# First queries' low parts by VectorE, maxima in two transfers, values around the gelu burst, bias additions moved, unread products in the tail

## The chip, the cores and the metric

The kernel is one program on one of the eight cores of a Trainium2 chip. The metric is the time of one execution on the device in microseconds; the median over runs counts. All engine names are the chip's: TensorE (PE) multiplies into PSUM, VectorE (DVE) and ScalarE (ACT) work elementwise and read PSUM, GpSimd (POOL) works on SBUF alone, SyncE (SP) issues nearly all transfers (DMAs).

## The reference

Four batches of 512 tokens with 256 features go through four residual steps. Each is gated by a tanh and begins with a layer norm. The heart of it:

```
x = x + tanh(g_xattn[0]) * xattn0(layernorm(x), ctx, ctx)     # 16 heads of 16, softmax over 512 keys
x = x + tanh(g_ffn[0])   * moe(layernorm(x))                   # router over 8 experts, the best 2, each x @ W[e]
x = x + tanh(g_xattn[1]) * xattn1(layernorm(x), ctx, ctx)
x = x + tanh(g_ffn[1])   * ffn(layernorm(x))                   # quantised x @ w1.T, gelu, quantised h @ w2.T

q, k, v = query @ Wq.T + bq, key @ Wk.T + bk, value @ Wv.T + bv
out = softmax(q k.T / sqrt(16)) v @ Wo.T + bo
```

The feed-forward network has 1024 hidden features. Weights are rounded to -1, 0 and 1 times a scale, activations to 8 bits with a scale for each token.

## The kernel before, in words

The work is cut into eight passes p = 0 to 7: two layers times four batches. A pass has 16 steps G (four groups of four heads, each in four token tiles), and each step has two halves, so that a pass has 32 slots. `table()` writes out one list for the whole program. In each slot stand: scores `S` of a step six steps ahead (`LEAD`), the transposed scores `T` of this step, whose exponential ScalarE takes (L991), and in every second slot the product with the values `PV` (L782). All other work (projections, layer norms, output projection, router and experts, feed-forward) is put into slots by hand in `work_table()`: `put(p, s, ...)` puts it into slot s of pass p. Every engine walks through the same list and executes its own part of each entry, in this order and never in another. So each engine has a fixed queue, and semaphores hold it at each entry until its inputs are there.

Queries and keys are split into a high part and a low part, so that products of them are exact enough. `SPLIT` does this for 128 features of a projection: TensorE multiplies (L707), ScalarE writes a full copy `qf` (L938) and a rounded high part (L939), GpSimd subtracts one from the other for the low part (L574), and SP stores both to the scratch tensors `qd` or `kd`. `RELOAD` brings them back from there, arranged by heads, as `qs` and `ks` (L521).

The softmax needs the maximum of each row. VectorE takes it from the scores (L1171, 512 reductions in the program). For each group of heads GpSimd splits the maxima into two parts (`M`, L648, L651), TensorE transposes them (`MT`, L791), ScalarE copies them (L1007), and SP moves them with four transfers into rows of `qs` (L531), for each part and each half of the partitions one. The transposed product `T` (L768) then subtracts them by itself.

`VV` (L727, L1125) makes the values of the next pass. In passes 5 to 7 all four gelu products `F1` (L879, L1042) of the previous batch stand together in slot 16, since ScalarE has to load another function table for the gelu and load the exponential's table after it (1.28 us each). They use the PSUM tiles of the scores, `psT` for the even ones and `psS` for the odd ones, and the scores wait until the gelus have read them. In passes 5 and 6 two `VV` stand among them; pass 7 has none.

`BIAS` adds the output projection's bias, scaled by the gate, to the residual `xs` on GpSimd (L621); `BOB` scales that bias on VectorE (L1087). After pass 7 comes a tail for the last batch alone: output projection (L819), layer norm, quantisation `XQ` and `XI`, transposes `XB` (L858), four gelu products, and for each of four tiles the rounding `HQ`, `HS`, transposes `HT` (L889) and the second product `F2` (L897).

The bookkeeping that the change touches on TensorE is the table of what frees each of the two banks of `psX`, which all the small work shares in turn:

```
freed = {"WS": (v_scale, 1, 1), "SPLIT": (a_split, 2, 2), "VV": (v_vv, 1, 1), "XT": (a_xt, 1, 1), "OT": (a_ot, 1, 1),
```

Of the kernel before, what the change touches and what calls it, by code (L numbers as in the profile page):

```python
# [19 lines left out]
F32 = mybir.dt.float32  # L20
F32R = mybir.dt.float32r
# [60 lines left out]
def work_table():  # L82
# [16 lines left out]
    put(lead, 24, ("BOB", ()))  # L99
    put(lead, 25, ("BIAS", (0, 0)))  # L100
# [3 lines left out]
    put(0, 0, ("SPLIT", ("Q", 1, 0)), ("LD", ("x3",)), ("BIAS", (1, 0)))  # L104
# [7 lines left out]
    put(0, 8, ("VV", (1, 0)), ("BIAS", (2, 0)), ("LD", ("moe0",)))  # L112
# [6 lines left out]
    put(0, 14, ("VV", (1, 1)), ("BIAS", (3, 0)))  # L119
# [16 lines left out]
    for p in range(1, NP):  # L136
# [35 lines left out]
        else:  # L172
# [19 lines left out]
    put(NP, 5, ("XQ", (0, 2)), ("LNN", (b, 2, 4)), ("XI", (0, 2)), ("XB", (0, 2)), ("XQ", (2, 4)), ("XI", (2, 4)))  # L192
    put(NP, 5, ("F1", (0,)), ("XB", (2, 4)), ("F1", (1,)), ("F1", (2,)), ("F1", (3,)))
# [56 lines left out]
def build(nc, x, ctxT, g_xattn, g_ffn, Wq, bq, Wk, bk, Wv, bv, Wo, bo, rw, rb, ew, w1, w2, out):  # L250
    with ExitStack() as ctx:
# [143 lines left out]
        v_xn = sem("v_xn")  # L395
        v_norm = sem("v_norm")
# [27 lines left out]
        for kind, args in table():  # L424
            if kind == "SPLIT":
                split_no[args] = len(split_no)

# [16 lines left out]
        def _(sp):  # L444
# [52 lines left out]
            def split(what, p, c):  # L497
                i = n("SPLIT")
                at, pr = (kd if what == "K" else qd)[p], parts[:, i % 2]
                if due(p_split, i + 1):  # L500
                    sp.wait_ge(p_split, i + 1)
# [22 lines left out]
            def max_rows(g):  # L524
# [21 lines left out]
        def _(pool):  # L546
# [23 lines left out]
            def split(what, p, c):  # L570
                i = n("SPLIT")
                if due(a_split, 2 * (i + 1)):
                    pool.wait_ge(a_split, 2 * (i + 1))
# [95 lines left out]
        def _(pe):  # L669
# [3 lines left out]
            freed = {"WS": (v_scale, 1, 1), "SPLIT": (a_split, 2, 2), "VV": (v_vv, 1, 1), "XT": (a_xt, 1, 1), "OT": (a_ot, 1, 1),  # L673
# [17 lines left out]
            def split(what, p, c):  # L691
                l = p // B
                o = bank("SPLIT")
                if what == "Q":
# [703 lines left out]
```

## Time and profile before

| | us |
|---|---|
| median of 3 runs | 766.89 |
| fastest and slowest of them | 765.59 and 769.69 |
| the profiled execution | 766.51 |
| its span, first to last instruction | 764.7 |
| TensorE busy in it | 676.7 (88%) |
| VectorE busy | 530.5 (69%) |
| ScalarE busy | 446.8 (58%) |
| GpSimd busy | 167.0 (22%) |
| mean granted clock of TensorE | 0.960 of full |

The profiled execution is one run; all lengths and times within the program come from it, counted from the span's start. A busy TensorE is not one at its peak, because products overlap and their ends are modelled. The engines run side by side: a length counts towards the time only where the others wait for it.

### The profile page before, as it was taken

What the parts mean: (1) busy time and instruction counts of PE and PEld (TensorE: products, weight loads), DVE (VectorE), ACT (ScalarE), POOL (GpSimd) and SP (SyncE); (2) the same over time, 40 slices, a digit from 0 to 9 for tenths busy, and PEclk for the clock granted to TensorE, in tenths of its full rate; (3) what the DMA queues carried; (4) which work ended last, traced back from release to release, by engine and by line L of the source; (5) the groups of instructions that cost most, each with busy time, mean ns of one, the idle gap of its engine ahead of it and who ended that gap; (6) DMA issues with size and microseconds to landing.
All of it is one profiled execution on the core that took longest, in us unless ns stands there. A gap on an engine that the chain in (4) does not pass through costs nothing.

```text
span 764.7 us, 10140 instructions
## 1 busy us (share of the span) xinstructions
PE 676.7 (88%) x3550; PEld 323.6 (42%) x3554; DVE 530.5 (69%) x1138; ACT 446.8 (58%) x572; POOL 167.0 (22%) x302
## 2 busy tenths in 40 slices
PE   4799999998999999998999989998889789987746
PEld 2433333344544445444554445443344344432324
DVE  3467876578886688868787688864786768775234
ACT  2227666773346633664336734468776778568746
POOL 6325222630010310121101410113210311021132
PEclk9769999999999999999999999999999999969987
DMA  7848578512120601123220321216032312200000
GB/s 239 230 117 317 180 232 267 158 34 52 42 43 29 166 18 26 46 108 84 43 43 30 122 47 42 43 70 207 10 83 64 94 39 64 43 2 9 21 0 28
DMA packets 39922, 66.74 MB, mean 87 GB/s; under 512 B 6080, under 2 KB 14784, under 8 KB 39616
## 3 DMA queue, kind: packets, MB, share of 16 engines
q1 hardware_dynamic: 39024, 65.57, 30.0%
q8 instruction: 28, 0.46, 0.3%
q10 hardware_dynamic: 848, 0.53, 0.2%
q14 instruction: 22, 0.18, 0.1%
HBM read 38.29 MB, written 27.26 MB: 86 GB/s over the span
## 4 chain that ended last, share of the span: by engine, by line
PE 56%; DVE 14%; ACT 12%; issue 9%; POOL 6%; DMA 2%; SPq 0%; POOLq 0%; DVEq 0%; ACTq 0%
PE psO L782 10%; PE psS L754 7%; PE psX L707 7%; DVE mx L1171 6%; PE psT L768 6%; PE psX L843 5%; PE psX L819 4%; ACT pt L991 4%; PE psX L844 4%; PE psX L845 4%; PE psX L727 3%; ACT qf L938 2%; DVE xs L1302 2%; POOL parts L574 2%; ACT parts L939 2%
## 5 line engine op out<-in xcount | busy, mean ns | idle before, releaser
L991 ACT ACTIVATE pt<-psT 128x1024 f32<-128x1024 f32 x256 | 261.8, 1023 | 217.1 <-PE psT L768 214.7
L1171 DVE TENSOR_REDUCE mx<-psS 128x1 f32<-128x512 f32 x512 | 325.1, 681 | 87.4 <-PE psS L754 86.1
L754 PE MATMUL psS<-ks,qs 48*128 48x512 f32 x512 | 153.8, 516 | 18.9 <-DVE mx L1171 13.2
L782 PE MATMUL psO<-pt,vg 128*32 128x512 f32 x1024 | 140.4, 621 | 0.1
L768 PE MATMUL psT<-qs,ks 50*128 50x512 f32 x512 | 118.2, 431 | 9.6 <-ACT pt L991 8.2
L754 PEld LDWEIGHTS psS<-ks,qs 48*128 48x128 f32 x512 | 61.0, 191 | 138.2 <-issue 72.3
L1302 DVE SCALAR_TENSOR_TENSOR xs<-psX,coef,xs 128x256 f32<-128x256 f32 x128 | 61.8, 483 | 31.8 <-PE psX L845 28.5
L574 POOL TENSOR_TENSOR parts<-qf,parts 128x512 fp32r<-128x512 f32 x32 | 40.8, 1275 | 158.7 <-ACT parts L939 158.7
L768 PEld LDWEIGHTS psT<-qs,ks 50*128 50x128 f32 x512 | 52.2, 189 | 29.4 <-ACT pt L991 25.8
L843 PE MATMUL psX<-moeh,xh 128*128 128x512 f32 x128 | 57.1, 446 | 5.3 <-DVE xs L1302 5.3
L844 PE MATMUL psX<-moel,xh 128*128 128x512 f32 x128 | 50.7, 396 | 0.0
L845 PE MATMUL psX<-moeh,xl 128*128 128x512 f32 x128 | 50.2, 392 | 0.0
L843 PEld LDWEIGHTS psX<-moeh,xh 128*128 128x128 f32 x128 | 23.9, 187 | 43.9 <-DVE xs L1302 23.8
L707 PE MATMUL psX<-ctxb,wk 128*128 128x512 f32 x64 | 34.4, 667 | 7.7 <-DMA wk<-in_Wk 7.7
L648 POOL CAST mp<-mx 128x16 fp32r<-128x16 f32 x32 | 6.4, 199 | 158.6 <-DVE mx L1171 157.7
L948 ACT ACTIVATE xn<-xs,lnw 128x256 f32<-128x256 f32 x60 | 31.8, 591 | 14.2 <-POOL lnw L610 14.1
L663 POOL TENSOR_SCALAR hh<-hh,am 128x1024 f32<-128x1024 f32 x16 | 18.0, 1123 | 95.2 <-DVE am L1343 95.2
L782 PEld LDWEIGHTS psO<-pt,vg 128*32 128x32 f32 x1024 | 20.3, 108 | 43.5 <-issue 42.5
L707 PE MATMUL psX<-xnt,wq 128*128 128x512 f32 x64 | 32.2, 630 | 1.3 <-ACT xnt L961 0.8
L819 PE MATMUL psX<-wo,ont 128*128 128x256 f32 x128 | 31.6, 391 | 0.8 <-ACT ont L984 0.8
L1100 DVE BATCH_NORM_STATS2 st<-xs 128x6 f32<-128x256 f32 x64 | 26.4, 413 | 7.4 <-DMA xs<-in_x 6.7
L1125 DVE TENSOR_TENSOR vg<-psX,bvb 128x512 f32<-128x512 f32 x16 | 11.0, 691 | 29.1 <-PE psX L727 29.1
(128 smaller groups left out, 748.9 us busy)
## 6 DMA issues: line engine op xcount, KB each, us to landing
ks<-kd SPq DMA_DIRECT2D x64, 192.0 KB, 3.7
qs<-qd SPq DMA_DIRECT2D x64, 192.0 KB, 4.5
kd<-parts SPq DMA_DIRECT2D x16, 512.0 KB, 3.1
qd<-parts SPq DMA_DIRECT2D x16, 512.0 KB, 2.7
kd<-parts SPq DMA_DIRECT2D x16, 256.0 KB, 3.8
qd<-parts SPq DMA_DIRECT2D x16, 256.0 KB, 3.7
ctxb<-in_ctxT SPq DMA_DIRECT2D x7, 512.0 KB, 3.5
xs<-in_x SPq DMA_DIRECT2D x4, 512.0 KB, 6.4
```

The source lines that it names most:

```text
L574: g.tensor_tensor(parts[:, i % 2, 1, :].bitcast(F32R), qf[:, i % 2, :], parts[:, i % 2, 0, :], ALU.subtract).then_inc(p_split, 1)
L707: i = mm(o, w[:, k, c * P:(c + 1) * P], src[:, k, :], start=k == 0, stop=k == NC - 1)
L754: mm(psS[:, i % 3, :], qs[at:at + KR, 2 * g + a, k * P:(k + 1) * P], ks[at:at + KR, 2 * g + a, :], start=True, stop=True).then_inc(pe_s, 1)
L768: i = mm(psT[:, r, :], ks[at:at + KR + MP, 2 * g + half, k * P:(k + 1) * P], qs[at:at + KR + MP, 2 * g + half, :], start=True, stop=True)
L782: i = mm(psO[32 * j:32 * j + 32, :], vg[:, p % 2, k, g * GH + j, :], pt[:, s % RING, j, :], start=k == 0, stop=k == NT - 1, tile_position= ...
L819: i = mm(o[:, t * D:(t + 1) * D], ont[:, k, tt * P:(tt + 1) * P], wo[l][:, k, :], start=k == 0, stop=k == NC - 1)
L843: mm(o, xh[:, k, tok], moeh[:, k, at], start=k == 0, stop=False)
L844: mm(o, xh[:, k, tok], moel[:, k, at], start=False, stop=False)
L845: i = mm(o, xl[:, k, tok], moeh[:, k, at], start=False, stop=k == NC - 1)
L991: a(pt[:, G % RING, 2 * half:2 * half + 2, :], psT[:], ACT.Exp, scale=SCALE).then_inc(a_exp, 1)
L1171: v.tensor_reduce(mx[:, w // GH % 2, r, col:col + 1], psS[:, i % 3, :], AX.X, ALU.max).then_inc(v_max, 1)
L1302: v.scalar_tensor_tensor(out=xs[:, b, t, :], in0=o[:, k * D:(k + 1) * D], scalar=coef[:, t, e:e + 1], in1=xs[:, b, t, :], op0=ALU.mult, op ...
```

## The change

It has five parts.

1. The low parts of the first pass's queries (`SPLIT` with ("Q", 0, 0) and ("Q", 0, 1)) are made by VectorE straight from PSUM: product plus bias minus high part, in one instruction. ScalarE's full copy and GpSimd's subtraction are left out for these two.
2. The transposed maxima of a group go to `qs` with two transfers in place of four. Each writes one row in both halves of the partitions.
3. In passes 5 and 6 one `VV` stands ahead of the four gelu products and one behind them.
4. `BOB` moves from slot 24 to slot 31 of the lead-in, and the four `BIAS` of layer 0 from slots 25 of the lead-in, 0, 8 and 14 of pass 0 to slots 5, 13, 21 and 29 of pass 0.
5. In the tail TensorE makes 46 products of 128x512 (29, 4, 4 and 9) whose result no one reads.

```diff
-    put(lead, 24, ("BOB", ()))
-    put(lead, 25, ("BIAS", (0, 0)))
+    put(lead, 31, ("BOB", ()))
...
+    for b in range(B):
+        put(0, 5 + 8 * b, ("BIAS", (b, 0)))
...
-            for t in range(NT):
-                put(p, 16, ("F1", (t,)))
-                if p < NP - 1 and t in (1, 2):
-                    put(p, 16, ("VV", (p + 1, t - 1)))
+            burst = [("F1", (t,)) for t in range(NT)]
+            if p < NP - 1:
+                burst = [("VV", (p + 1, 0))] + burst + [("VV", (p + 1, 1))]
+            put(p, 16, *burst)
...
-    put(NP, 5, ("XQ", (0, 2)), ("LNN", (b, 2, 4)), ("XI", (0, 2)), ("XB", (0, 2)), ("XQ", (2, 4)), ("XI", (2, 4)))
-    put(NP, 5, ("F1", (0,)), ("XB", (2, 4)), ("F1", (1,)), ("F1", (2,)), ("F1", (3,)))
+    put(NP, 4, ("BUSY", (29,)))
+    put(NP, 5, ("XQ", (0, 2)), ("LNN", (b, 2, 4)), ("XI", (0, 2)), ("XB", (0, 2)), ("BUSY", (4,)), ("XQ", (2, 4)), ("XI", (2, 4)))
+    put(NP, 5, ("F1", (0,)), ("XB", (2, 4)), ("BUSY", (4,)), ("F1", (1,)), ("F1", (2,)), ("F1", (3,)),
+        ("BUSY", (9,)))
...
                 for k in range(MP):
-                    for half in range(2):
-                        row, src = HALF * half + KR + k, k * GH * NT + half * 2 * NT
-                        sp.dma_start(qs[row:row + 1, 2 * g:2 * g + 2, :].bitcast(F32)
-                                     .rearrange("p h (t q) -> p (h t) q", q=P),
-                                     mt[src:src + 2 * NT, i % 2, :]).then_inc(d_m[i % 2], 16)
+                    sp.dma_start(qs[KR + k:HALF + KR + k + 1:HALF, 2 * g:2 * g + 2, :].bitcast(F32)
+                                 .rearrange("p h (t q) -> p (h t) q", q=P),
+                                 mt[k * GH * NT:(k + 1) * GH * NT, i % 2, :]).then_inc(d_m[i % 2], 16)
...
+                last[b] = (v_split, dve_parts(i + 1)) if by_dve(i) else (a_split, act_parts(i + 1))
...
+            def keep_busy(k):
+                if due(a_oe, n("OE")):
+                    pe.wait_ge(a_oe, n("OE"))
+                if due(v_quant, 16):
+                    pe.wait_ge(v_quant, 16)
+                for i in range(k):
+                    mm(psO[:], identb[:], w1q[:, 0, 0:S], start=True, stop=True)
...
-                a(qf[:, i % 2, :], o, ACT.Identity, bias=bias).then_inc(a_split, 1)
+                if not by_dve(i):
+                    if due(p_split, pool_parts(i - 1)):
+                        act.wait_ge(p_split, pool_parts(i - 1))
+                    a(qf[:, i % 2, :], o, ACT.Identity, bias=bias).then_inc(a_split, 1)
                 a(parts[:, i % 2, 0, :].bitcast(F32R), o, ACT.Identity, bias=bias).then_inc(a_split, 1)
...
+                if due(pe_split, i + 1):
+                    dve.wait_ge(pe_split, i + 1)
+                if due(a_split, act_parts(i + 1)):
+                    dve.wait_ge(a_split, act_parts(i + 1))
+                v.scalar_tensor_tensor(out=parts[:, i % 2, 1, :].bitcast(F32R), in0=bank(), scalar=bqc[:, 0, c:c + 1],
+                                       in1=parts[:, i % 2, 0, :], op0=ALU.add, op1=ALU.subtract).then_inc(v_split, 1)
```

`by_dve(i)` is true for the two splits of part 1; `dve_parts`, `pool_parts` and `act_parts` count the instructions that each engine has made up to a split.

What the change moves on the engines, in the order in which their instructions stand (line numbers are each program's own). First VectorE in the opening, before the change, from the normalised first batch (`xn`) over the second batch's statistics (`st`, `mv`) to the maxima (`mx`):

```order
L1111 TENSOR_SCALAR xn<-xs,lnw 128x256 x4
L1100 BN_STATS st<-xs 128x6
L1105 BN_AGGR mv<-st 128x2
...
L1125 TENSOR_TENSOR vg<-psX,bvb 128x32x16 x2
L1171 TENSOR_REDUCE mx<-psS 128x1 x10
L1087 TENSOR_SCALAR bob<-bob,gt 128x256 x2
L1171 TENSOR_REDUCE mx<-psS 128x1 x16
```

And after the change, at the same place:

```order
L1144 TENSOR_SCALAR xn<-xs,lnw 128x256 x4
L1171 SCALAR_TENSOR_TENSOR parts<-psX,bqc,parts 128x512
L1133 BN_STATS st<-xs 128x6
L1138 BN_AGGR mv<-st 128x2
...
L1171 SCALAR_TENSOR_TENSOR parts<-psX,bqc,parts 128x512
L1158 TENSOR_TENSOR vg<-psX,bvb 128x32x16 x2
L1215 TENSOR_REDUCE mx<-psS 128x1 x24
L1120 TENSOR_SCALAR bob<-bob,gt 128x256 x2
L1215 TENSOR_REDUCE mx<-psS 128x1 x2
```

The first low part has come ahead of the four pairs of statistics, the second between them and the values, and the scaling of the bias has moved from behind the 10th maximum to behind the 24th.

Next TensorE at the gelu burst of pass 5, before the change (`xit` are the transposed inputs, `wv,ctxb` a `VV`):

```order
L768 MATMUL psT<-qs,ks 128x512 x2
L879 MATMUL psT<-w1q,xit 128x512 x4
L879 MATMUL psS<-w1q,xit 128x512 x4
L727 MATMUL psX<-wv,ctxb 128x256 x4
L879 MATMUL psT<-w1q,xit 128x512 x4
L727 MATMUL psX<-wv,ctxb 128x256 x4
L879 MATMUL psS<-w1q,xit 128x512 x4
L754 MATMUL psS<-ks,qs 128x512 x2
```

And after it:

```order
L792 MATMUL psT<-qs,ks 128x512 x2
L751 MATMUL psX<-wv,ctxb 128x256 x4
L903 MATMUL psT<-w1q,xit 128x512 x4
L903 MATMUL psS<-w1q,xit 128x512 x4
L903 MATMUL psT<-w1q,xit 128x512 x4
L903 MATMUL psS<-w1q,xit 128x512 x4
L751 MATMUL psX<-wv,ctxb 128x256 x4
L778 MATMUL psS<-ks,qs 128x512 x2
```

The two projections of values have gone from among the gelu products to both sides of them.

Last TensorE in the tail, where before the change the transposes of the quantised inputs (`identb,xi`) follow the output projection at once:

```order
L819 MATMUL psX<-wo,ont 128x256 x8
L858 MATMUL psX<-identb,xi 128x128 x4
L879 MATMUL psT<-w1q,xit 128x512 x4
L858 MATMUL psX<-identb,xi 128x128 x4
L879 MATMUL psS<-w1q,xit 128x512 x4
```

And after it:

```order
L843 MATMUL psX<-wo,ont 128x256 x8
L930 MATMUL psO<-w1q,identb 128x512 x29
L882 MATMUL psX<-identb,xi 128x128 x4
L930 MATMUL psO<-w1q,identb 128x512 x4
L903 MATMUL psT<-w1q,xit 128x512 x4
L882 MATMUL psX<-identb,xi 128x128 x4
L930 MATMUL psO<-w1q,identb 128x512 x4
L903 MATMUL psS<-w1q,xit 128x512 x4
```

The unread products (`psO<-w1q,identb`) have come in between; nine more stand behind the last gelu product.

## Rows read from the trace of the kernel before

**Rows 1.** The page: the clock in 40 slices, and the chain that ended last by engine.
```profile
PEclk9769999999999999999999999999999999969987
...
PE 56%; DVE 14%; ACT 12%; issue 9%; POOL 6%; DMA 2%; SPq 0%; POOLq 0%; DVEq 0%; ACTq 0%
```

**Rows 2.** The chain that ended last, opening of the program: start us, us, what.
```profile
19.98 1.28 POOL parts L574
...
29.61 0.84 PE psS L754 x2
...
36.42 0.60 DVE bob L1087 x2
```

**Rows 3.** Timeline, 14 to 29 us: start, length, engine, line, operation, idle before it.
```profile
14.52 0.41 DVE L1100 BATCH_NORM_STATS2 st<-xs 128x6 f32<-128x256 f32 x1
...
16.55 0.18 DVE L1105 BATCH_NORM_AGGREGATE mv<-st 128x2 f32<-128x6 f32 x1
...
19.22 0.68 ACT L939 ACTIVATE parts<-psX,bqc 128x512 fp32r<-128x512 f32 x1
...
26.43 1.07 PE L738 MATMUL psX<-identf,xn 128*128 128x128 f32 x8 [2.67 <-ACT xn L948]
```

**Rows 4.** Groups by shape, VectorE: count, busy us, mean ns, idle before.
```profile
L1198 DVE SCALAR_TENSOR_TENSOR xs<-psX,gt,xs 128x512 f32<-128x512 f32 x16 | 12.0, 748 | 24.6 <-PE psX L819 24.6
```

**Rows 5.** Timeline, maxima moved and first products that read them, 42 and 211 us.
```profile
42.03 2.84 SPq L531 DMA_DIRECT2D qs<-mt  x4
...
46.06 0.29 PEld L768 LDWEIGHTS psT<-qs,ks 50*128 50x128 f32 x2 [0.19 <-DMA qs<-mt]
...
211.59 2.69 SPq L531 DMA_DIRECT2D qs<-mt  x4
...
221.62 0.40 PE L768 MATMUL psT<-qs,ks 50*128 50x512 f32 x2
```

**Rows 6.** Timeline, gelu burst of pass 6, with values inside.
```profile
609.01 1.02 ACT L991 ACTIVATE pt<-psT 128x1024 f32<-128x1024 f32 x1
...
611.83 1.89 PE L727 MATMUL psX<-wv,ctxb 128*128 128x256 f32 x8
...
618.91 1.29 DVE L1171 TENSOR_REDUCE mx<-psS 128x1 f32<-128x512 f32 x2 [1.88 <-PE psS L754]
...
619.63 1.03 ACT L991 ACTIVATE pt<-psT 128x1024 f32<-128x1024 f32 x1
```

**Rows 7.** Busy us by stretch: PE, PEld, DVE, ACT, POOL, PEclk, DMA share, GB/s.
```profile
620.00:640.00 20.00, 17.46 (x129) 8.17 (x127) 19.09 (x41) 16.18 (x19) 3.79 (x5) 1.00 0.23 55
```

**Rows 8.** Timeline, gelu burst of pass 7, without values.
```profile
687.86 1.02 ACT L991 ACTIVATE pt<-psT 128x1024 f32<-128x1024 f32 x1
...
692.37 1.04 PE L879 MATMUL psS<-w1q,xit 128*128 128x512 bf16 x4
...
694.58 1.28 ACT L991 ACT_TABLE_LOAD   x1
```

**Rows 9.** Timeline, the same exponential in passes 6 and 7.
```profile
597.07 1.02 ACT L991 ACTIVATE pt<-psT 128x1024 f32<-128x1024 f32 x1 [1.22 <-PE psT L768]
...
673.64 1.02 ACT L991 ACTIVATE pt<-psT 128x1024 f32<-128x1024 f32 x1 [1.22 <-PE psT L768]
```

**Rows 10.** The chain of the tail, 724 to 765 us, by line.
```profile
by line: PE psX L897 8.9%; ACT hh L1042 7.9%; PE psT L879 7.0%; issue 6.9%; ACT hq L1053 5.3%; PE psX L889 5.1%; PE psX L819 4.8%; PE psS L879 4.5%; POOL lnw L594 3.6%; ACT hqt L1067 3.6%; PE psO L782 2.7%; ACT xit L1031 2.7%; ACT ont L984 
```

**Rows 11.** Timeline, TensorE's long pause in the tail.
```profile
730.20 3.69 PE L819 MATMUL psX<-wo,ont 128*128 128x256 f32 x16 [0.83 <-ACT ont L984]
...
741.32 0.59 PE L858 MATMUL psX<-identb,xi 128*128 128x128 bf16 x4 [7.43 <-ACT xi L1021]
```

**Rows 12.** Busy us by stretch, columns as in Rows 7.
```profile
674.00:688.00 14.00, 13.11 (x53) 4.41 (x45) 8.50 (x17) 8.95 (x13) 3.23 (x11) 0.52 0.01 2
...
739.00:749.00 10.00, 5.23 (x18) 2.32 (x20) 3.46 (x13) 5.54 (x8) 3.27 (x7) 0.50 0.01 2
```

**Rows 13.** Timeline, one bias addition on GpSimd.
```profile
52.58 2.34 POOL L621 TENSOR_TENSOR xs<-xs,bob 128x1024 f32<-128x1024 f32 x1
```

More of the change, by code:

```diff
@@ L103, in work_table @@
         st(0, 5 + t, 3, t)
-    put(0, 0, ("SPLIT", ("Q", 1, 0)), ("LD", ("x3",)), ("BIAS", (1, 0)))
+    put(0, 0, ("SPLIT", ("Q", 1, 0)), ("LD", ("x3",)))
     put(0, 1, ("LD", ("w1",)))
@@ L118, in work_table @@
     put(0, 13, ("WS", ()))
-    put(0, 14, ("VV", (1, 1)), ("BIAS", (3, 0)))
+    put(0, 14, ("VV", (1, 1)))
     pair(0, 16, "SPLIT", "Q", 3, step=2)
@@ L395, in build @@
         v_xn = sem("v_xn")
+        v_split = sem("v_split")
         v_norm = sem("v_norm")
@@ L426, in build, with by_dve, dve_parts, pool_parts @@
                 split_no[args] = len(split_no)
+        def by_dve(i):
+            return i in (split_no["Q", 0, 0], split_no["Q", 0, 1])
+        def dve_parts(i):
+            return sum(by_dve(k) for k in range(i))
+        def pool_parts(i):
+            return i - dve_parts(i)
+        def act_parts(i):
+            return 2 * i - dve_parts(i)
         def ctx_of(p):
@@ L499, in split @@
                 at, pr = (kd if what == "K" else qd)[p], parts[:, i % 2]
-                if due(p_split, i + 1):
-                    sp.wait_ge(p_split, i + 1)
+                if by_dve(i):
+                    if due(v_split, dve_parts(i + 1)):
+                        sp.wait_ge(v_split, dve_parts(i + 1))
+                else:
+                    if due(p_split, pool_parts(i + 1)):
+                        sp.wait_ge(p_split, pool_parts(i + 1))
                 if what == "Q":
@@ L571, in split @@
                 i = n("SPLIT")
-                if due(a_split, 2 * (i + 1)):
-                    pool.wait_ge(a_split, 2 * (i + 1))
+                if by_dve(i):
+                    return
+                if due(a_split, act_parts(i + 1)):
+                    pool.wait_ge(a_split, act_parts(i + 1))
                 g.tensor_tensor(parts[:, i % 2, 1, :].bitcast(F32R), qf[:, i % 2, :], parts[:, i % 2, 0, :],
@@ L692, in split @@
                 l = p // B
+                i = n("SPLIT")
+                b = n.piece() % 2
                 o = bank("SPLIT")
+                last[b] = (v_split, dve_parts(i + 1)) if by_dve(i) else (a_split, act_parts(i + 1))
                 if what == "Q":
@@ L759, in t_pair @@
                 if k == 0 and half == 0:
-                    if due(d_m[no % 2], 64 * (no // 2 + 1)):
-                        pe.wait_ge(d_m[no % 2], 64 * (no // 2 + 1))
+                    if due(d_m[no % 2], 32 * (no // 2 + 1)):
+                        pe.wait_ge(d_m[no % 2], 32 * (no // 2 + 1))
                 if due(a_exp, n("T")):
@@ L1004, in mt_ @@
                     act.wait_ge(pe_mt, i + 1)
-                if due(d_m[i % 2], 64 * (i // 2)):
-                    act.wait_ge(d_m[i % 2], 64 * (i // 2))
+                if due(d_m[i % 2], 32 * (i // 2)):
+                    act.wait_ge(d_m[i % 2], 32 * (i // 2))
                 a(mt[:, i % 2, :].bitcast(F32R), bank()[0:MP * GH * NT, 0:P], ACT.Copy).then_inc(a_mt, 1)
@@ L1128, in vv, with split @@
                                 ALU.add).then_inc(v_vv, 1)
+            def split(what, p, c):
+                i = n("SPLIT")
+                if not by_dve(i):
+                    return
+                if due(pe_split, i + 1):
+                    dve.wait_ge(pe_split, i + 1)
+                if due(a_split, act_parts(i + 1)):
+                    dve.wait_ge(a_split, act_parts(i + 1))
+                v.scalar_tensor_tensor(out=parts[:, i % 2, 1, :].bitcast(F32R), in0=bank(), scalar=bqc[:, 0, c:c + 1],
+                                       in1=parts[:, i % 2, 0, :], op0=ALU.add, op1=ALU.subtract).then_inc(v_split, 1)
             def raw(k):
@@ L1354, in f2 @@
                                        in1=xs[:, b, t, :], op0=ALU.mult, op1=ALU.add).then_inc(v_f2, 1)
-            walk({"BOB": scale_bo, "ST": stats, "LNV": normalise, "VV": vv, "ABS": abs_sum, "WS": scales, "QUANT": quant, "S": maxima,
+            walk({"BOB": scale_bo, "ST": stats, "LNV": normalise, "SPLIT": split, "VV": vv, "ABS": abs_sum, "WS": scales, "QUANT": quant, "S": maxima,
                   "NT": norm, "OP": op, "R1": router1, "R2": router2, "R3": router3, "R4": router4, "ME": experts, "XQ": xq,
```

8 lines of the change are left out of this document (3 added, 5 removed).

## The prediction

> **What bounds the kernel now.** I read the page first. The chain that ended last spends 56% of the span on TensorE, 14% on VectorE, 12% on ScalarE and 6% on GpSimd, and the clock row shows TensorE at its upper level (2.4 GHz) nearly everywhere [rows 1]. It is lower in slices 2 and 3 (the opening), in slice 36 (669 to 688 us) and in the last two (the tail). So the steady passes belong to TensorE, and a saving of waits counts only where TensorE itself stands still or runs at 1.2 GHz. Of the change's places, four could be such: the opening, the two gelu bursts that carry value projections, the transfers of the maxima, and the tail.
>
> In the opening the chain runs over GpSimd's subtraction for the first queries, their store, their reload, and the first scores at 29.61 [rows 2]. Then VectorE's maxima set the pace, with BOB's two scalings (0.60) between them, up to the first transposed product at 46.06 [rows 2, 5]. In the tail TensorE stands idle for 7.43 us before the transposes at 741.32, and works at a granted clock of 0.50 from 739 to 749 [rows 11, 12].
>
> **First queries' low parts.** The subtraction ended at 21.26 (19.98 + 1.28) [rows 2]. Now ScalarE writes one copy instead of two. Its high part takes 0.68 [rows 3] and can start where the full copy did, some 0.6 before 19.22, thus ends at 19.3. VectorE then adds the bias and subtracts. The same kind of instruction on 128x512 out of PSUM takes 0.75 [rows 4], so it ends at 20.1. The store leaves 1.2 earlier.
>
> VectorE executes in order, and this instruction stands before the second batch's statistics, which ran from 14.52 to 16.73 in VectorE's free time [rows 3]. They now run from 20.1 to 22.3. Their normalisation on GpSimd could start at 21.3, behind the subtraction [rows 2]; it now starts at 22.3, about 1.0 later. What hangs on it is the transposes at 26.43 (1.07 long) [rows 3]: they move to 27.4 and end at 28.5. TensorE issues the first scores behind them. These were at 29.61; the store would allow 28.4, the transposes allow 28.55. **Gain 1.05**, with 1.2 as the upper end. The cover (2.1 us between transposes and scores) is then used up; the lower end is 0.5, if the statistics or the normalisation run later by as much again. The second low part stands behind those statistics, holds its PSUM bank until 23 and delays the second value projection, which has until 27.4.
>
> **BOB and the bias additions.** BOB leaves the place between the 10th and 11th maximum and stands behind the 24th. There the first transposed product may already start, and TensorE next does a projection while VectorE has two maxima left. **Gain 0.6** [rows 2]. The four additions on GpSimd cost 2.34 each [rows 13], the same number as before. They move to slots 5, 13, 21 and 29 of pass 0, each just behind the splitting of a group's maxima (slots 3, 11, 19, 27) and so as far as can be from the next. There they stand ahead of one low-part subtraction each; the first also waits for ScalarE's normalisation. What waits behind them is that subtraction and its store, and ScalarE only two projections later. I take 0. Without that cover each would cost up to 2.34.
>
> **Maxima in two transfers.** SP issues 128 transfers now and 64 after. Four take 2.69 to issue [rows 5], so two should take 1.35. Who waits? In a steady pass the four are issued by 214.3 and the first product that reads their rows comes at 221.62 [rows 5], a cover of 7.3 us. The saving there is worth 0. Only the very first group is near: issued 42.03 to 44.87, and the product at 46.06 was released by that landing, 1.2 after the last issue [rows 5]. VectorE's chain reaches the same point within 0.2. Both gates move: the maxima are ready 1.65 earlier, and issuing is done 1.4 earlier still. So the first product should follow VectorE's chain; between 0 and 0.2 more.
>
> The row shows four transfers landing 1.2 after the last issue. The Trainium skill's page DMA: Bandwidth & Descriptors (section on why a DMA increments its semaphore by 16) says that the number of engines is the largest up to 16 that divides the slowest dimension of both sides. By it the old form (8 rows on each side) used eight engines, and the new one (2 partitions against 16 rows) uses two, each with eight rows in a line. By that rule issuing gets cheaper and landing slower; no row here times the new form. By the row alone the sum has 0 for this edit, by the rule anything up to the whole 7.3 cover would still be 0, and only the first group could lose some tenths.
>
> **Values at both ends of the burst.** Pass 6 has two projections inside, pass 7 has none. I count from the start of the last exponential. In pass 7 the last gelu ends 6.72 later (694.58 - 687.86) [rows 8]. In pass 6 the next exponential, which comes 1.28 plus a few hundredths after the last gelu, starts 10.62 later (619.63 - 609.01) [rows 6], so the last gelu ends 9.3 later. The two projections inside cost ScalarE 2.6. Now the first stands before the first gelu product: it can start when the last transposed product ends, runs some 1.73 (1.89 with the filling of the array [rows 6]) while ScalarE still has its exponential (1.02) and the table load (1.28), and makes the first gelu 0.25 late. The second stands behind the last product, which in pass 7 ends 5.55 after the exponential's start (692.37 + 1.04 - 687.86) [rows 8]. So it ends at 5.55 + 0.25 + 1.73 = 7.5, and scores and transposed products follow (0.40 for such a pair [rows 5], so 0.7 to 0.8). They are ready at 8.25, the table at 6.72 + 0.25 + 1.28 = 8.25, and the exponential starts at 8.27. **ScalarE gains 10.62 - 8.27 = 2.35.** VectorE has a copy out of PSUM to make before its next maximum (0.75 by [rows 4]), so that starts at 7.5 + 0.75 = 8.25 and not at 9.90 (618.91 - 609.01) [rows 6]: **gain 1.65**. In the 20 us that follow VectorE is busy for 19.09, ScalarE for 16.18 [rows 7], so VectorE sets most of the pace. I take 1.8 for each, **3.6 for the two** (passes 5 and 6), between 3.3 and 4.7.
>
> **Unread products in the tail.** Twenty-nine products follow the output projection, which ends at 733.9 [rows 11], in the pause. Four of this size took 1.04 at the upper level [rows 8], so 29 take 6.3 to 7.5 and end at 740.2 to 741.4. The transposes want TensorE at 741.3. They cost about nothing if the clock is still up when they begin. On the chain of the tail (40.7 us) the gelu products are 7.0 + 4.5%, or 4.7 us; the transposes of the hidden rows 5.1%, or 2.1; the last products 8.9%, or 3.6 [rows 10]. At the upper level two gelu products stand before a gelu, 2.1 instead of 4.7, and one more gelu of 1.1 joins the chain: -1.5. The small transposes and weight loads around them give 0.5. In the second half -0.9 for transposes and -0.7 for one product at the lower level; ScalarE then sets the pace and takes back 0.6. **Gain 3.0**, of 3.6 at most. The groups of 4 and 4 stand ahead of a first product and of a second one, whose inputs come from ScalarE a short copy later; at 0.9 each, 0.2 of delay is in the sum. The 9 at the end (1.9) hide behind two gelus. The lower end is 1.0, if the clock falls again before the last products.
>
> **Sum.** 1.05 + 0.6 + 0 + 0 + 3.6 + 3.0 = 8.25. The profiled execution took 766.5 (its span 764.7 plus 1.8 around it) and the median of the runs is 766.9. So 758.3 against the profiled one, and **758.6** for the median.
>
> **Rivals.**
> 1. The tail does not gain (chance 0.14). The clock falls before the products come, or they start at the lower level, where 29 take twice as long, up to 12.6, and end at 746.5, 5 us after the transposes want the engine. For it: they only keep up what is there, and the tail ahead of them has gaps [rows 11]. Against: the projection before them is 3.7 us without a gap at the upper level. Gain 0 to -3 in the tail: 762 to 765.
> 2. The bursts give little (0.08), if TensorE or VectorE takes back the time in the following pass: 766.9 - 1.65 - 3.0 - 0.5 = 761.8. Against it stands pass 7, where the burst without projections is 2.6 shorter.
> 3. The dips fall elsewhere (0.12 with an effect over 2 us). From 674 to 688 TensorE ran at 0.52 though it was busy for 13.11 of 14 [rows 12]; pass 6 at the same place ran at full clock. The same two exponentials lie 11.94 apart in pass 6 and 14.22 in pass 7 [rows 6, 8, 9]: a dip costs 2.3 or more, since pass 7 also lacks a projection (1.9). All the work shifts against it here. Without it 755 to 756, with one more 761 to 763.
> 4. The maxima come too late (0.03), the case on the other side: two engines carrying sixteen rows one after the other, behind the reloads. It decides from a landing 7.3 + 1.35 us later than now [rows 5]; from there on each microsecond costs one for each of 32 groups. A landing 9 us later gives 766.9 - 8.25 + 32 x 0.35, or 770.
>
> The forecast itself has 0.63. **Range 754.5 to 762.5**: below it the lost dip, above it the case without the tail's gain. What this kernel's measurement tells from no change is about 0.5%, 3.8 us. Over 763.1 is only the bad half of rival 1, part of 4, and several losses at once: faster 0.90, same 0.07, slower 0.03.
>
> **What would show it.** The first scores near 28.5 and the first transposed product near 44.4. The last exponential before the table load and the next one 8.3 apart in passes 5 and 6, with no gap in TensorE ahead of the third gelu product. SP's groups of two near 1.35 and no wait of transposed products for them. Clock 1.00 from 739 on and the last gelu about 2 us nearer to the transposes. I am wrong if scores come after 29.2, if the unread products end after 741.5, or if a new dip stands in pass 5 or 6.

## The result, and the profile after

The changed kernel takes **763.94 us** (median of 20 runs, 757.05 to 769.72), the kernel before 768.4 beside it (20 runs, 764.61 to 770.45). The ratio is **0.9945, 95% interval 0.9923 to 0.9967**, or 4.2 us less where I forecast 8.25. The forecast of 758.6 stood on 766.89, the median of three runs of the kernel before; beside the changed kernel that median is 768.4, so 1.5 of the 5.3 us between 758.6 and 763.94 come from the base, and the rest is gain that did not come. I call "low time" the time at TensorE's lower level: two times (1 - mean granted clock) times 765 us. It is 56 us as a mean over the runs of after (two slow ones left out, as in all ratios) and 63 over the 35 runs of before that stand beside e1 to e4 below.

First the opening, by the timeline of TensorE and then of ScalarE in the kernel after (start, length, what ran, in brackets the idle time ahead and what ended it). These answer to [rows 2, 3 and 5].

```profile
27.47 1.06 PE L762 MATMUL psX<-identf,xn 128*128 128x128 f32 x8 [2.48 <-ACT xn L981]
28.49 1.22 PE L778 MATMUL psS<-ks,qs 48*128 48x512 f32 x3
...
43.96 1.21 PE L792 MATMUL psT<-qs,ks 50*128 50x512 f32 x2
45.11 3.78 PE L731 MATMUL psX<-xnt,wq 128*128 128x512 f32 x4
```

```profile
48.92 0.69 ACT L971 ACTIVATE qf<-psX,bqc 128x512 f32<-128x512 f32 x1 [2.69 <-PE psX L731]
```

The scores start at 28.49 (29.61 before). The first two transposed products start at 43.96 and end at 45.17, where before they ended at 46.86, so that the exponential behind them comes 1.7 earlier. The projection behind them runs at 1.2 GHz for its whole 3.78 (3.18 before), so part is given back: the same copy stood at 50.01 before and is 1.1 earlier now.

The burst of pass 6, by the timelines of ScalarE, VectorE and TensorE of after, answering to [rows 6]:

```profile
610.04 1.02 ACT L1024 ACTIVATE pt<-psT 128x1024 f32<-128x1024 f32 x1
611.08 1.28 ACT L1075 ACT_TABLE_LOAD   x1
...
617.09 1.28 ACT L1024 ACT_TABLE_LOAD   x1
618.38 1.02 ACT L1024 ACTIVATE pt<-psT 128x1024 f32<-128x1024 f32 x1
```

```profile
617.68 0.69 DVE L1158 TENSOR_TENSOR vg<-psX,bvb 128x512 f32<-128x512 f32 x1 [5.15 <-PE psX L751]
618.29 1.28 DVE L1215 TENSOR_REDUCE mx<-psS 128x1 f32<-128x512 f32 x2
619.48 1.21 DVE L1377 TENSOR_REDUCE am<-hh 128x1 f32<-128x1024 f32 x1
...
621.30 1.28 DVE L1215 TENSOR_REDUCE mx<-psS 128x1 f32<-128x512 f32 x2
```

```profile
620.67 0.49 PE L778 MATMUL psS<-ks,qs 48*128 48x512 f32 x1
622.04 0.53 PE L778 MATMUL psS<-ks,qs 48*128 48x512 f32 x1 [0.88 <-DVE mx L1215]
622.04 0.96 PE L792 MATMUL psT<-qs,ks 50*128 50x512 f32 x2
622.93 1.93 PE L806 MATMUL psO<-pt,vg 128*32 128x512 f32 x8
```

From exponential to exponential it is 8.34 (618.38 - 610.04; 8.33 in pass 5), where I forecast 8.27 and before had 10.62. But VectorE, idle for 5.15 inside the burst, now has the copy of the values, two maxima and the first hidden tile's quantisation maximum (`HQ`, L1377) in a row. TensorE waits 0.88 for it, where before it waited 0.32, and the product with the values at 622.93 takes 1.93 instead of 1.06: the clock has fallen. The same two places in the trace before:

```profile
622.67 0.50 PE L754 MATMUL psS<-ks,qs 48*128 48x512 f32 x1 [0.32 <-DVE mx L1171]
...
623.34 1.06 PE L782 MATMUL psO<-pt,vg 128*32 128x512 f32 x8
```

The fall shows in the windows of after (busy time of each engine with the number of instructions, then the granted clock):

```profile
616.00:619.00 3.00, 3.00 (x20) 1.56 (x18) 1.32 (x3) 2.97 (x4) 0.00 (x0) 1.00 0.00 0
619.00:622.00 3.00, 2.03 (x13) 0.97 (x9) 2.90 (x8) 1.99 (x3) 0.52 (x1) 1.00 0.01 3
622.00:625.00 3.00, 2.96 (x13) 0.70 (x15) 2.36 (x5) 1.96 (x2) 1.02 (x3) 0.56 0.00 0
625.00:628.00 3.00, 3.00 (x17) 1.71 (x17) 2.31 (x3) 2.04 (x4) 0.00 (x0) 0.50 0.00 0
```

Pass 5 is the same in kind: a pause of 0.88 ahead of 542.81, then low clock from 544, for 3.4 us instead of the 6.8 of pass 6. The trace before had no low stretch behind either burst.

The tail, by the timeline of TensorE after and one window, answering to [rows 11, 12]:

```profile
732.99 3.69 PE L843 MATMUL psX<-wo,ont 128*128 128x256 f32 x16 [0.83 <-ACT ont L1017]
736.73 6.21 PE L930 MATMUL psO<-w1q,identb 128*128 128x512 bf16 x28
744.09 0.38 PE L882 MATMUL psX<-identb,xi 128*128 128x128 bf16 x4 [1.15 <-ACT xi L1054]
```

```profile
739.00:749.00 10.00, 8.13 (x43) 3.41 (x42) 4.07 (x13) 5.68 (x9) 4.42 (x15) 1.00 0.00 0
```

The clock is 1.00 where it was 0.50. From the output projection to the last instruction on VectorE it is 29.8 us (732.99 to 762.80) against 32.4 (730.20 to 762.58): 2.6 gained. At the places touched the opening gains 1.1, each burst 1.65 (VectorE's next maximum) and the tail 2.6, and yet the span is that of before (764.9 and 764.7). What a burst gains can be followed further, to the first exponential of the next pass. From the last exponential ahead of the table load to that one it was 41.49 in pass 5 (530.89 to 572.38) and 41.47 in pass 6 (609.01 to 650.48). It is now 40.59 (530.81 to 571.40) and 42.06 (610.04 to 652.10): of the 3.3 of the two bursts 0.3 is left there. The 17 us of low time that stood in the tail are gone, but the mean granted clock is 0.958 against 0.960, so as much stands elsewhere. One such stretch, of 6.8 us from 595, lies in pass 6 ahead of its burst and makes the way there 2.0 longer (38.64 from 571.40 to 610.04, against 36.63 before). Over the runs of after, time and low time go together (correlation 0.95): each us of low time goes with 0.34 us.

### The profile page after: what moved, and what is told of

Same layout as the page of the kernel before. It is cut to its first block, busy times and chain, and to the rows that moved or that the text cites. A ratio compares the mean times of both kernels' runs of the same rounds, so it can differ in the third digit from the quotient of the medians.

```text
span 764.9 us, 10167 instructions
## 1 busy us (share of the span) xinstructions
PE 691.0 (90%) x3595; PEld 327.5 (43%) x3600; DVE 533.3 (70%) x1140; ACT 445.5 (58%) x570; POOL 164.3 (21%) x300
## 4 chain that ended last, share of the span: by engine, by line
PE 59%; DVE 14%; ACT 11%; issue 9%; POOL 8%; POOLq 0%; DVEq 0%; ACTq 0%
PE psO L806 11%; PE psS L778 8%; PE psX L731 7%; PE psT L792 6%; PE psX L867 5%; DVE mx L1215 5%; PE psX L843 4%; PE psX L868 4%; PE psX L869 4%; PE psX L751 3%; ACT pt L1024 3%; POOL parts L595 2%; DVE xs L1346 2%; ACT qf L971 2%; ACT parts L972 1%
## 5 line engine op out<-in xcount | busy, mean ns | idle before, releaser
L806 PE MATMUL psO<-pt,vg 128*32 128x512 f32 x1024 | 142.0, 627 | 0.1
L1346 DVE SCALAR_TENSOR_TENSOR xs<-psX,coef,xs 128x256 f32<-128x256 f32 x128 | 61.8, 483 | 32.4 <-PE psX L869 29.2
L595 POOL TENSOR_TENSOR parts<-qf,parts 128x512 fp32r<-128x512 f32 x30 | 38.4, 1280 | 152.5 <-ACT parts L972 152.5
L731 PE MATMUL psX<-ctxb,wk 128*128 128x512 f32 x64 | 36.6, 705 | 7.3 <-DMA wk<-in_Wk 7.3
L751 PE MATMUL psX<-wv,ctxb 128*128 128x256 f32 x128 | 33.0, 403 | 0.8 <-DVE parts L1171 0.8
L612 POOL TENSOR_SCALAR lnw<-mv 128x4 f32<-128x4 f32 (+1 forms) x17 | 3.9, 229 | 126.3 <-DVE mv L1138 125.7
```

What stands on the lines that cost most here:

```text
L731: i = mm(o, w[:, k, c * P:(c + 1) * P], src[:, k, :], start=k == 0, stop=k == NC - 1)
L751: i = mm(o[:, t * D:(t + 1) * D], ctxb[:, p % 2, k, (2 * half + t) * P:(2 * half + t + 1) * P], wv[l][:, k, :], start=k == 0, stop=k == NC ...
L806: i = mm(psO[32 * j:32 * j + 32, :], vg[:, p % 2, k, g * GH + j, :], pt[:, s % RING, j, :], start=k == 0, stop=k == NT - 1, tile_position= ...
L1346: v.scalar_tensor_tensor(out=xs[:, b, t, :], in0=o[:, k * D:(k + 1) * D], scalar=coef[:, t, e:e + 1], in1=xs[:, b, t, :], op0=ALU.mult, op ...
```

## The experiments

Low time is the mean over a kernel's runs. "Before" is the median of the kernel before on the same chip in the same session. e1 to e4 are before with one part of the change, e5 to e8 vary after, e9 to e12 build on e7.

| kernel | us | before | ratio (95% interval) | low time |
|---|---|---|---|---|
| e1 tail alone | 765.84 | 768.24 | 0.9967 (0.9940 to 0.9994) | 48 |
| e2 bursts alone | 767.96 | 768.24 | 0.9986 (0.9956 to 1.0016) | 73 |
| e3 opening alone | 766.10 | 768.24 | 0.9987 (0.9962 to 1.0012) | 59 |
| e4 maxima alone | 768.06 | 768.24 | 1.0003 (0.9974 to 1.0031) | 64 |
| e5 after, old bursts | 763.82 | 769.59 | 0.9931 (0.9905 to 0.9957) | 45 |
| e6 after, pause filled | 762.62 | 769.59 | 0.9921 (0.9891 to 0.9952) | 55 |
| e7 after, one `HQ` in burst | 759.82 | 769.59 | 0.9865 (0.9836 to 0.9895) | 51 |
| e8 after, two `HQ` in burst | 760.50 | 769.59 | 0.9880 (0.9858 to 0.9903) | 53 |
| e9 e7 and more pauses filled | 760.99 | 766.36 | 0.9918 (0.9886 to 0.9951) | 49 |
| e10 e7 and opening filled | 757.62 | 766.36 | 0.9879 (0.9848 to 0.9909) | 36 |
| e11 e10 and two in lead-in steps | 759.95 | 766.36 | 0.9898 (0.9864 to 0.9932) | 24 |
| e12 e10 and one in lead-in steps | 756.73 | 770.70 | 0.9828 (0.9774 to 0.9881) | 25 |

The low time of before is 63 beside e1 to e4, 66 beside e5 to e8, 60 beside e9 to e11 and 70 beside e12: compare low times across these groups with care.

**e1: the tail alone.** Only the `BUSY` entries and `keep_busy` of the change.

```diff
+    put(NP, 4, ("BUSY", (29,)))
```

> Before, with the unread products of the tail alone. Theory A (each part gives what I counted, and a part of the gain is eaten by clock dips that stand in new places of passes 1, 5, 6 and 7): the tail shows the clock at 1.00 and the time is 2.5 to 3 us lower, since nothing ahead of the tail moves. Rival B (the trace of after overstates the tail; the full clock there was luck): 0 to 1 us lower, with low clock again after 739. Rival C (a dip that is held off in one place comes in another, whatever is done): the tail is at full clock and the time still less than 1.5 us lower, with about as much time at the low clock as before (64 us) in the whole span.

Measured 2.5 us less (0.5 to 4.6), with 1.00 from 739 to 759 and 48 us of low time against 63. Rival B wanted low clock there and rival C as much low time as before, so both fall; by the time alone neither would. In this one trace the tail from the last exponential on is 2.5 shorter than before (38.3 against 40.8).

**e2: the bursts alone.**

```diff
+                burst = [("VV", (p + 1, 0))] + burst + [("VV", (p + 1, 1))]
```

> Before, with the value projections at both ends of the gelu burst alone. If the bursts cost clock dips in passes 5 to 7 (theory A's suspect): exponential to exponential 8.3 in passes 5 and 6, new low stretches within 30 us behind a burst, and the time only 0 to 1.5 us lower, or higher. If the bursts are innocent: the same 8.3, no new low stretches in passes 5 and 6, and 3 to 4 us lower.

Measured 1.1 us less (-1.2 to 3.4), not told apart from nothing, though the exponentials are 8.34 and 8.46 apart. Low time grew by 10 us, the only part of the change that raises it by more than 1. The windows of e2 behind the burst of pass 6 look as in after, and the timeline has a pause of 0.86 in pass 5:

```profile
624.00:626.00 2.00, 1.13 (x5) 0.48 (x4) 1.90 (x8) 0.36 (x1) 1.12 (x1) 1.00 0.01 4
626.00:628.00 2.00, 2.00 (x11) 0.66 (x12) 1.69 (x4) 1.88 (x2) 0.20 (x1) 0.62 0.00 0
628.00:630.00 2.00, 2.00 (x15) 1.10 (x13) 1.62 (x3) 1.43 (x4) 0.22 (x1) 0.53 0.00 0
```

```profile
547.18 0.50 PE L777 MATMUL psS<-ks,qs 48*128 48x512 f32 x1 [0.86 <-DVE mx L1214]
547.84 1.86 PE L805 MATMUL psO<-pt,vg 128*32 128x512 f32 x8
```

In both passes 3.4 us of low clock follow. To the first exponential of the next pass it is 40.60 and 40.67, together 1.7 less than before. At 0.34 each, ten us of low time would cost 3.4, an estimate from the runs of after; what the bursts gain while the clock holds is read from traces under e7 and e8.

**e3: the opening alone**, `by_dve` with its semaphores, and the moves of `BOB` and `BIAS`.

```diff
+    put(lead, 31, ("BOB", ()))
+            return i in (split_no["Q", 0, 0], split_no["Q", 0, 1])
```

> Before, with the opening alone (low parts by VectorE, scaling and bias additions moved). If the sizes I counted are right and no dip moves: 1.3 to 1.7 us lower, first scores 1.1 earlier, first transposed product 1.2 to 1.7 earlier. If the low clock up to 49 us gives part back: 0.5 to 1 lower. If the shift of everything behind it places new dips: 0 to 3 higher or lower, with new low stretches in passes that the edit does not touch.

Measured 1.0 less by the ratio, between -2.9 and +0.9. The forecast of 1.65 and its lower variants all fit.

**e4: the maxima alone.**

```diff
+                    sp.dma_start(qs[KR + k:HALF + KR + k + 1:HALF, 2 * g:2 * g + 2, :].bitcast(F32)
```

> Before, with the maxima in two transfers alone. By my prediction: no change (0, at most 0.3 lower for the first group). If fewer issues on SyncE let reloads and stores come earlier and that changes how work falls: up to 1 us lower. If the landing of these transfers holds TensorE somewhere and so lets its clock fall: higher, with waits of transposed products for them.

No change, as forecast. The four parts add up to -2.5 - 1.1 - 1.0 + 0.2 = -4.4, the whole change gave -4.2: no sign that they disturb each other, though each term is known to about 2 us only.

**e5: after without its bursts.**

```diff
-            burst = [("F1", (t,)) for t in range(NT)]
-            if p < NP - 1:
-                burst = [("VV", (p + 1, 0))] + burst + [("VV", (p + 1, 1))]
-            put(p, 16, *burst)
+            for t in range(NT):
+                put(p, 16, ("F1", (t,)))
+                if p < NP - 1 and t in (1, 2):
+                    put(p, 16, ("VV", (p + 1, t - 1)))
```

> After, with the gelu burst as before (value projections between the gelu products); opening, maxima and tail stay changed. Theory A (the burst saves 3.6 us of waits, and its new pause behind the burst costs about 10 us of low clock, worth 3): time within 1 us of after (763.9), at about 47 us of low clock instead of 57, and no low stretch between 541 and 552 or 620 and 632. Rival (low stretches are luck, the same with any kernel): as much low clock as after, and 3 to 4 us slower than after.

As theory A has it: taking the bursts back costs nothing that could be measured (0.9931 against 0.9945) and removes 11 us of low time. The clock holds behind both bursts, with a wait of 0.34, about the old one:

```profile
544.42 0.50 PE L778 MATMUL psS<-ks,qs 48*128 48x512 f32 x1 [0.34 <-DVE mx L1215]
```

**e6: the pause filled.** Three products that no one reads, in the free bank of `psX`. `hold` makes them, and the reader of that bank is waited for.

```diff
+            if p < NP - 1:
+                put(p, 18, ("HOLD", (3,)))
...
+            def hold(k):
+                b = n.piece() % 2
...
+                for i in range(k):
+                    mm(psX[:, b, :], identb[:], w1q[:, 0, 0:S], start=True, stop=True)
```

> After, with three more products that no one reads in passes 5 and 6, where TensorE waits 0.88 us for VectorE's maximum, two steps behind the burst (622.0 in after). Theory A1 (that pause is what lets the clock fall): full clock up to at least 15 us behind the burst in both passes, low clock down by 5 to 10 us, time 1.5 to 3.5 us lower than after. Rival (the clock falls for another reason, e.g. by the work of the burst itself): the low stretch stays, time as after or up to 0.5 higher.

The profile shows what A1 asks for. The wait behind the products is 0.22, the product with the values takes 1.07, and no low stretch stands behind either burst:

```profile
539.39 0.81 PE L931 MATMUL psX<-w1q,identb 128*128 128x512 bf16 x3
540.13 0.50 PE L780 MATMUL psS<-ks,qs 48*128 48x512 f32 x1
540.85 0.50 PE L780 MATMUL psS<-ks,qs 48*128 48x512 f32 x1 [0.22 <-DVE mx L1224]
540.85 0.73 PE L794 MATMUL psT<-qs,ks 50*128 50x512 f32 x2
541.51 1.07 PE L808 MATMUL psO<-pt,vg 128*32 128x512 f32 x8
```

Over all traces kept, the place behind the burst goes one way. With the new burst alone (after and e2) the clock fell in four of four. It held in the ten with the old burst (before, e1, e3, e4, e5), in the two with the pause filled (e6) and in all twelve of e7 to e12, in which the pause does not arise.

The time of the whole program is weaker evidence. The ratio lies 0.0024 under that of after, within the intervals, and the mean low time did not fall (55, with 44 to 69 in single runs).

**e7 and e8: the cause of the pause moved.** One or two `HQ` stand in the burst, ahead of the second `VV`, where VectorE idles.

```diff
-                burst = [("VV", (p + 1, 0))] + burst + [("VV", (p + 1, 1))]
+                burst = [("VV", (p + 1, 0))] + burst + [("HQ", (t,)) for t in range(1)] + [("VV", (p + 1, 1))]
...
+                if p == NP - 1 or t >= 1:
+                    put(p, 17 + 3 * t, ("HQ", (t,)))
```

> After, with the first hidden tile's quantisation maximum (VectorE, 1.9 us with its four small steps) put into the burst of passes 5 and 6, ahead of the second value projection, where VectorE stands idle for 5.15 us. Theory A1: VectorE is then no longer late two steps behind the burst, TensorE's pause of 0.88 goes, the clock holds, and both gains come: 3 to 5 us lower than after, 759 to 761. Rival (clock dips are luck): about 1 us lower, from the shorter queue of VectorE alone.

> As the kernel with one such maximum in the burst, with the second tile's as well (3.8 us together in the idle 5.15). Theory A1: the same or up to 1.5 us lower than with one. Against it: the second ends just when the value projection's product does, so it could make that copy and the first maximum behind the burst up to 0.5 late in each pass; then the same as with one, or 1 us higher.

e7 comes out at 0.9865, 0.8% or 6 us under after, more than the 3 to 5 expected. e8 equals it. The timelines of VectorE and TensorE in e7: the maximum lies inside the burst, and the scores two steps behind it wait for no one.

```profile
537.40 1.22 DVE L1378 TENSOR_REDUCE am<-hh 128x1 f32<-128x1024 f32 x1 [1.32 <-ACT hh L1076]
...
541.23 0.69 DVE L1159 TENSOR_TENSOR vg<-psX,bvb 128x512 f32<-128x512 f32 x1 [1.92 <-PE psX L752]
541.84 1.28 DVE L1216 TENSOR_REDUCE mx<-psS 128x1 f32<-128x512 f32 x2
543.32 1.29 DVE L1216 TENSOR_REDUCE mx<-psS 128x1 f32<-128x512 f32 x2 [0.20 <-PE psS L779]
```

```profile
544.22 0.50 PE L779 MATMUL psS<-ks,qs 48*128 48x512 f32 x2
544.64 0.50 PE L793 MATMUL psT<-qs,ks 50*128 50x512 f32 x2
545.07 1.07 PE L807 MATMUL psO<-pt,vg 128*32 128x512 f32 x8
```

Averaged over the runs the low time fell by 5 us only, so the clock can't be all of it. How the gain divides can be read from the traces, again from the last exponential ahead of the table load to the first of the next pass. The ends in pass 6, by ScalarE's timelines of before, after, e6 and e7:

```profile
650.48 1.02 ACT L991 ACTIVATE pt<-psT 128x1024 f32<-128x1024 f32 x1 [0.68 <-PE psT L768]
652.10 1.02 ACT L1024 ACTIVATE pt<-psT 128x1024 f32<-128x1024 f32 x1 [0.68 <-PE psT L792]
645.65 1.02 ACT L1033 ACTIVATE pt<-psT 128x1024 f32<-128x1024 f32 x1 [0.68 <-PE psT L794]
647.14 1.02 ACT L1025 ACTIVATE pt<-psT 128x1024 f32<-128x1024 f32 x1 [0.68 <-PE psT L793]
```

| kernel | pass 5 | pass 6 | both |
|---|---|---|---|
| before, old burst | 41.49 | 41.47 | 82.96 |
| e5, old burst | 41.44 | 41.47 | 82.91 |
| after, new burst, clock falls | 40.59 | 42.06 | 82.65 |
| e2, new burst, clock falls | 40.60 | 40.67 | 81.27 |
| e6, pause filled, clock holds | 39.91 | 39.80 | 79.71 |
| e7, `HQ` in the burst | 38.47 | 38.46 | 76.93 |

These are single executions, but kernels with the same burst and no low stretch agree within 0.15 here: e1, e3 and e4 have 41.45 to 41.52, e8 to e12 38.44 to 38.57. So with the clock held the new bursts gain 3.25 (before to e6), the low stretches cost 2.9 of it in after and 1.6 in e2, and `HQ` in the burst gives 2.8 more (e6 to e7) by VectorE's shorter queue behind it, which I had priced at 1. The 5.7 between after and e7 are the 6 us.

**e9: the pauses ahead of other low stretches filled.**

```diff
+        put(p, 9, ("HOLD", (2,)))
+        put(p, 10, ("HOLD", (2,)))
...
+        if slot == 2 * H * 5 + 12:
+            out.append(("HOLD", (4,)))
```

> As the kernel with one hidden maximum in the burst, with unread products where TensorE stands still ahead of the low stretches that every kernel so far shares: two in slots 9 and 10 of passes 1 to 7 (the steps behind the output projection, TensorE busy for 1.5 of 2 us, twice in a row) and four ahead of the transposed maxima at slot 12 of pass 5 (pause of 1.26). If pauses of this kind are what lets the clock fall: no low stretch near 143 to 182, 521 and 669 to 683, 15 to 20 us less low clock, and 3 to 6 us lower. If they delay the scores that VectorE waits for: up to 0.5 per pass higher, 3 in all. Rival (dips are luck): the same low clock, same time.

A miss. The low time is that of e7, and the ratio 0.5% above e7's (on another chip). The low stretches moved more than they went. In pass 7 the clock held to 678 and was low for 6.8 us, in e7 for 13.7 from 669; the one of pass 5 came at 532 instead of 522. Those of pass 1 stood at 143 and 170 instead of 161 and 178, and two more at 351 and 358, where e7 had none. What decides those stays open.

```profile
666.00:678.00 12.00, 9.63 (x55) 3.46 (x54) 10.23 (x25) 7.48 (x11) 2.93 (x11) 1.00 0.01 2
678.00:686.00 8.00, 7.18 (x32) 3.00 (x28) 4.23 (x8) 4.78 (x6) 1.78 (x4) 0.57 0.01 2
```

**e10 to e12: the opening filled.** Eight unread f32 products in pauses ahead of the first scores (e10), and two (e11) or one (e12) of half the width in each of the twelve steps of the lead-in.

```diff
+    for s in range(20, 32):
+        put(lead, s, ("SHORTLY", (1,)))
...
+    out += [("SPLIT", ("K", 0, 1)), ("EARLY", (3,))] + [("XT", (c,)) for c in range(NC)]
...
+    out += [("VV", (0, 0)), ("EARLY", (2,)), ("VV", (0, 1)), ("EARLY", (3,)), ("LNN", (1, 0, NT))] + [("XT", (c,)) for c in range(NC)]
```

> As the kernel with one hidden maximum in the burst, with eight unread 128x512 products of f32 (0.5 us each) in TensorE's pauses of the opening: three ahead of the first transposes, two and three around the second value projection. If the clock at the first scores depends on the pauses just ahead of them: full clock at 28.5, and 1 to 2 us lower. If the scores at VectorE's pace are themselves too thin to hold it: low clock starts some us later and stays to 48 all the same, 0 to 0.7 lower. If the products push the second projection or the transposes: up to 0.7 higher.

> As the kernel with eight unread products in the opening, with two more of 128x256 (0.25 each at the upper level) in each of the twelve steps of the lead-in, where VectorE needs 1.3 us for a step and TensorE 0.66. If the clock holds: full clock through the lead-in, the following projection 1.9 instead of 3.7, 1.5 to 3 us lower. If it falls all the same: a step then takes TensorE 1.2 + 1.0, so up to 0.9 more than VectorE needs, and the time is 5 to 10 us higher.

> As the kernel with eight unread products in the opening and two in each step of the lead-in, with one in place of two: in that kernel the clock held through the whole lead-in, but a step took 1.49 us instead of VectorE's 1.3. With one a step needs TensorE for 0.9. If the clock still holds: the lead-in at VectorE's 1.3, the following projection 1.9 instead of 3.8, 3 us lower than with two, so a ratio to before of 0.985 to 0.988. If one is too little: low clock from about 34 as with the eight alone, and TensorE then needs 1.2 + 0.55 for a step, 0.4 more than VectorE: a ratio of 0.99 to 0.995.

e10's ratio is that of e7 (on another chip), though its low time is 15 us less. One reason shows in the trace: the second transposes start at 29.14, 0.75 after their input is done at 28.39 (0.14 in after), because the unread products still run, so the filling costs 0.6 of what it gives. That low time also costs little where VectorE sets the pace is likely, but not shown apart. In e10 the clock is up when the scores start and falls at 34. With products in the steps it holds. The windows are those of e10, and then of e12:

```profile
34.00:38.00 4.00, 3.85 (x8) 1.65 (x7) 4.00 (x8) 0.00 (x0) 0.00 (x0) 0.59 1.08 342
46.00:50.00 4.00, 4.00 (x7) 1.17 (x4) 2.06 (x6) 1.02 (x1) 0.00 (x0) 0.50 0.01 2
```

```profile
34.00:38.00 4.00, 4.00 (x15) 2.11 (x14) 4.00 (x8) 0.00 (x0) 0.00 (x0) 1.00 1.11 347
46.00:50.00 4.00, 3.11 (x11) 1.09 (x10) 3.63 (x10) 3.06 (x4) 0.89 (x1) 1.00 0.00 0
```

With two products TensorE needs 1.49 for a step, and VectorE, for whom the steps are made, idles. With one a step takes 1.20, VectorE is busy for all of 34 to 38, and the projection behind takes 1.98 instead of 3.78. e12 is 3.2 us under e11 by the medians (on different chips), and at 756.73 the fastest of all: 1.7% under before. Its interval overlaps those of e7 and e10, so it is shown to beat both kernels of this study, but not them.

## Why the prediction was off

- **First queries' low parts (1.05): right.** Scores at 28.49, forecast 28.5, by the path forecast: the transposes at 27.47 set it, not the store.
- **`BOB` (0.6) and bias additions (0): right in place.** The transposed products start at 43.96 (forecast 44.4), and their exponential comes 1.7 earlier, as the two terms together had it (1.65). Of that 0.6 is given back, since the clock stayed low until 49 and the next projection took 3.78 instead of 3.18. Alone, the opening gave 1.0 with an interval too wide to say more.
- **Two transfers (0): right.** Issue takes 1.05 for two (1.35 forecast; the row of SyncE's timeline follows, answering to [rows 5]), and nothing waits for the landing.

```profile
210.66 1.05 SPq L550 DMA_DIRECT2D qs<-mt  x2
```

  A slower landing, which the prediction feared, hardly shows. In the trace of after the last data packet of the group at 210.66 ends 0.9 us after the issue does, where before it was 0.75 (211.59), so the whole move takes 1.9 instead of 3.4. Where other transfers are under way it is longer, up to 4.2 behind the issue, and still waited for by no one. By the rule of the Trainium skill's page DMA: Bandwidth & Descriptors (section on why a DMA increments its semaphore by 16) the new form uses two engines instead of eight. The trace agrees, if each engine adds one small packet: those under 512 B fell from 32 for four transfers to 4 for two, or from eight to two for each. e4 shows no cost (1.0003).
- **Bursts (3.6): the step that failed.** The burst shrank as worked out, to 8.34. I read [rows 7], VectorE busy for 19.09 of 20, as "VectorE sets most of the pace", and asked only what the saving would be worth at its pace. I did not ask what TensorE does meanwhile. The burst had been VectorE's time to catch up. Shortened by 2.3 it ends with VectorE late, since `HQ` stands in its queue behind the burst, and TensorE pauses for 0.88 instead of 0.32 and drops to 1.2 GHz. The sum put that at nothing. With the clock held the term is 3.25 (e6 against before), near the 3.6; the low stretches take back 2.9 in the trace of after and 1.6 in that of e2. Alone the term measured 1.1.
- **Tail (3.0): right.** Products end at 742.9. My sign of being wrong, an end after 741.5, is met by the letter, but only since everything ahead was 2.8 later; they still end ahead of the transposes at 744.09. 2.6 in the profile, 2.5 alone.
- **Rivals.** Rival 3 (dips fall elsewhere) is what happened. I gave it 0.12, because I took it as luck of the shift, worth one dip of 2.3 either way. Behind the bursts it had a cause: e2 alone has it, e5 without the bursts has not, e6 fills the pause and e7 removes it, and the stretch behind the burst goes each time. For the stretches elsewhere, such as that of 6.8 us from 595, no cause is shown. The test named in the prediction, a new dip in pass 5 or 6, was met.

The Trainium skill's page TensorE: Matmul & The Clock Gate (section HAM oscillation — how this bites in real kernels) prices throttled time at one half of its length. By that rule the 10 us of e2 would cost 5; the runs of after show 0.34 a us, and the 17 us of low time that left the tail were worth 2.6. The rows decide, and all lie under one half: behind the bursts 3.4 us of low clock cost 0.7 to 0.9, and 6.8 us 2.3 (after and e2 against e6). That it is less where another engine sets the pace is my reading, not measured by itself.

## What to carry to other kernels

Before shortening a stretch, look at which engine was catching up in it, and what stands next in that engine's queue. If it comes out late, the engine that you freed pauses, and TensorE can pay for the pause again in its clock. Move the late engine's own work into the stretch first: here moving one such piece measured 6 us (2.8 by the shorter queue, 2.9 by the clock, in the traces), and the whole change without it 4.2. Unread products paid only where they fitted into a pause that another engine sets. One too many in each step of the lead-in made a step 1.49 instead of 1.20, twelve times.

## What was not expected of the hardware

A pause of 0.88 us, with TensorE busy for 2.03 of 3 us around it, was followed by 6.8 us at the lower level in pass 6. In the trace before, at the same place, a pause of 0.32 was followed by none. The length of a pause alone does not decide: in the trace before one of 1.21 stands at the end of the burst, ahead of 618.37, and the clock held. Two pauses of 0.54 and 0.51 a little ahead of the burst of pass 6 stand in after (593.08 and 595.33) and in e5 (593.89 and 596.14) alike, behind the same work; in after the clock fell at 595, in e5 it held. Low stretches stand at other places in each kernel's execution, and single runs of one kernel differ by up to 32 us of low time, about 10 us of time: for a difference under 1% the mean granted clock of every run belongs beside its time. In two traces (e1 and e7) the clock was also low at 17 to 21 us and made the first queries' projection 5.1 to 5.2 long instead of 3.7, which moves all that follows by 1.5. In both, VectorE's normalised input came about 1 us late and TensorE had idled 3.3 to 3.4 us ahead of the transposes (1.75 in after). In e10 it came as late, but unread products filled that pause; the clock held and the projection took 3.67. No part of the change touches this place.
